# Conditional residual layer: weight-mixing bursts on TensorE in blocks of three, where they stood in blocks of two

## The reference

```python
masked_w = weight * mask[None, :, :]                  # (8, 512, 512)
w_bot = jnp.einsum('bg,got->bot', y, masked_w)         # one 512 x 512 matrix for each batch
return x + jnp.einsum('bnt,bot->bno', x, w_bot) + bias
```

## Time and profile before

| | us |
|---|---|
| median of 3 runs | 605.22 (604.99 to 605.52) |
| the profiled execution | 605.46 |
| its span, first to last instruction | 603.7 |

### The profile page before, as it was taken

How to read it: one execution, slowest core, us unless ns; L and a number is a source line. 1 busy time by engine, 2 the same in 40 slices (tenths; PEclk the granted TensorE clock), 3 DMA queues, 4 the chain that set the end, 5 groups by cost and what they waited for, 6 DMA issues and landing times.

```text
span 603.7 us, 14813 instructions
## 1 busy us (share of the span) xinstructions
PE 592.5 (98%) x6343; PEld 515.9 (85%) x6343; DVE 313.5 (52%) x524; ACT 142.0 (24%) x277; POOL 37.8 (6%) x34
## 2 busy tenths in 40 slices
PE   7899999999999999999999999999999999999998
PEld 6899988888888888888888888888888888888886
DVE  3565535455555555464465465555555555654342
ACT  4443322222222222222222222222222222220000
POOL 3430000000000113221000000000000000000000
PEclk9999999999999999999999999999999999999999
DMA  9976656686776899998766756766767766777952
GB/s 325 406 294 184 207 180 208 219 249 217 239 246 214 290 332 354 343 337 288 238 225 224 250 204 239 249 210 231 246 216 230 234 234 228 227 244 242 298 158 87
DMA packets 61089, 148.59 MB, mean 246 GB/s; under 512 B 6880, under 2 KB 9696, under 8 KB 61024
## 3 DMA queue, kind: packets, MB, share of 16 engines
q1 hardware_dynamic: 40176, 113.00, 57.3%
q10 hardware_dynamic: 20848, 34.64, 15.2%
HBM read 114.07 MB, written 33.55 MB: 245 GB/s over the span
## 4 chain that ended last, share of the span: by engine, by line
PE 95%; DMA 2%; DVE 1%; issue 1%; ACTq 0%; ACT 0%; DVEq 0%
PE ps L438 75%; PE ps L415 20%; DMA bias_sb<-in_bias 1%; DMA xs<-in_mask 1%; DVE wbot L321 0%; DVE staged L335 0%; PE ps L398 0%; ACTq L268 0%; DVE staged L349 0%; ACT wbot L263 0%; DVE wm L189 0%; DVE staged L354 0%; ACTq L277 0%; DVEq L161 0%; DVEq L346 0%
## 5 line engine op out<-in xcount | busy, mean ns | idle before, releaser
L438 PE MATMUL ps<-wbot,xs 128*128 128x256 f32 (+1 forms) x2176 | 459.3, 370 | 4.4 <-DVE wbot L321 3.7
L438 PEld LDWEIGHTS ps<-wbot,xs 128*128 128x128 f32 x2176 | 389.7, 190 | 59.2 <-issue 6.3
L321 DVE COPY wbot<-ps 128x512 f32<-128x512 f32 (+1 forms) x272 | 164.1, 649 | 183.8 <-PE ps L438 174.6
L263 ACT ACTIVATE wbot<-ps 128x512 f32<-128x512 f32 (+1 forms) x276 | 140.7, 568 | 400.7 <-PE ps L415 198.1
L415 PEld LDWEIGHTS ps<-y_sb,wm 32*128 32x128 f32 x4096 | 124.9, 190 | 21.7 <-issue 20.6
L415 PE MATMUL ps<-y_sb,wm 32*128 32x128 f32 x4096 | 137.5, 280 | 2.5 <-DVE wm L189 2.0
L349 DVE TENSOR_TENSOR staged<-ps,staged 128x512 f32<-128x512 f32 x111 | 76.3, 687 | 79.8 <-PE ps L438 79.8
L335 DVE TENSOR_TENSOR staged<-staged,bias_sb 128x512 f32<-128x512 f32 x112 | 76.4, 682 | 0.0
L189 POOL TENSOR_TENSOR wm<-wm,mask_sb 128x512 f32<-128x512 f32 x16 | 20.0, 1270 | 216.3 <-DMA mask_sb<-in_mask 216.3
L349 DVE TENSOR_TENSOR staged<-ps,bias_sb 128x256 f32<-128x256 f32 (+1 forms) x24 | 12.2, 510 | 15.5 <-PE ps L438 11.0
L189 POOL TENSOR_TENSOR wm<-wm,xs 128x512 f32<-128x512 f32 x14 | 17.6, 1274 | 21.7 <-DMA xs<-in_mask 21.4
(11 more groups left out here) (1 smaller groups left out, 0.1 us busy)
## 6 DMA issues: line engine op xcount, KB each, us to landing
xs<-in_x SPq DMA_DIRECT2D x128, 512.0 KB, 3.9
out<-staged ACTq DMA_DIRECT2D x119, 256.0 KB, 4.7
staged<-in_xn SPq DMA_DIRECT2D x112, 256.0 KB, 4.3
wm<-in_w SPq DMA_DIRECT2D x12, 512.0 KB, 6.4
mask_sb<-in_mask SPq DMA_DIRECT2D x8, 512.0 KB, 6.5
out<-staged ACTq DMA_DIRECT2D x18, 128.0 KB, 4.2
wm<-in_w SPq DMA_DIRECT2D x8, 256.0 KB, 6.8
xs<-in_mask SPq DMA_DIRECT2D x4, 512.0 KB, 13.4
```

The source lines that it names most:

```text
L263: eng.activation(tile_place(b, j, first, end), tile_sums(b, j, first, end), ACT.Copy).then_inc(s_ev_a, 1)
L321: eng.tensor_copy(tile_place(b, j, first, end), tile_sums(b, j, first, end)).then_inc(s_ev_v, 1)
L438: ins = eng.matmul(bank[:, at_h:at_h + width], xs[:, n % XRING, h, k, :], at, start=(k == 0), stop=(k == KT - 1))
```

## The change

`bursts_before` is the only function that changes. Before, every even `n` up to 112 had a block of two bursts (`n + 15` and `n + 16`), the first and the last block one burst. Now a unit has blocks ahead of six of its pieces: two bursts ahead of its first and its sixteenth, three ahead of its fourth, seventh, tenth and thirteenth. The blocks of three hold bursts `n + 14`, `n + 15` and `n + 16`. `n` = 0 keeps its single burst, and `n` = 112 has burst 127 alone. The lists `TAKEN` and `BANK_OF` and the loops of all engines follow from the function. The bursts, pieces and copies themselves are the same.

```diff
     n = m - EARLY
     if n == 0:
         return (CS,)
-    return () if n % 2 else tuple(b for b in (n + CS - 1, n + CS) if b < BURSTS)
+    first, count = {0: (-1, 2), 3: (1, 3), 6: (4, 3), 9: (7, 3), 12: (10, 3), 15: (13, 2)}.get(n % GROUPS, (0, 0))
+    at = n - n % GROUPS + CS + first
+    return tuple(b for b in range(at, at + count) if b < BURSTS)
```

## The result

The changed kernel took 629.62 us (median of 4 runs, 627.44 to 630.75) against 605.21 us: a ratio of 1.040 (1.038 to 1.041), 24.4 us more. I had forecast a loss, but 14.7 us of it, and 616 to 628 us as the range. The profiled execution took 629.95 us with a span of 628.2 us.

The account below looks back on a forecast made before the run. The prediction took PE's own instruction stream as the bound. Third-burst waits of 19.6 us less 4.9 us for fewer blocks gave +14.7 on 605.46 profiled, 620.2; the median, 0.24 lower, was forecast at 619.9 us, range 616 to 628.

Parts of the forecast that it names:

- What bounds the kernel: PE's own instruction stream: time taken out is an equal gain, and any wait by PE an equal loss.
- Part 1: Switches between pieces and bursts: 14 fewer blocks at 0.35 us each give back 4.9 us (2.2 to 7.3).
- Part 2, when tile 3's bank comes free: Third burst, steady state: VectorE's copy frees tile 3's bank at +2.67, and the tile starts 0.04 us later.
- all 26 left of the burst wait behind it: Third burst's rest starts 0.72 us late (0.58 in unit 0), 19.6 us over 28 blocks.
- Part 3: Copies, unit-start waits, output and staging loads: all covered, costed at nothing; the load's bias add comes about 11 us on.
- Rival 1: Third burst's 28 waits each end 0.24 us after the copy, not 0.04: 625.5 us; chance 0.12.
- Rival 2: Third burst's banks are free in time, so no wait at tile 3: 600.3 us; chance 0.05.
- Rival 3: Twenty-eight short holes in PE's stream lower the granted clock: about 641 us; chance 0.03.
- What would show it: Profile after: 28 new burst waits of 0.6 to 0.9 us, PE busy time and clock unchanged; new `in_xn` waits contradict.

Follow-up runs that it names:

- experiment 1: The changed kernel with the load into `staged` issued ahead of the second slice's weight and mask loads in SyncE's queue: 624.09 us, ratio 1.031.
- experiment 3: As experiment 1, but ahead of blocks of three VectorE adds the bias behind the copies of the block's first burst: 620.95 us, ratio 1.026.
- experiment 4: As experiment 1, but the first burst isn't copied out in 24 blocks of three, leaving out part of the layer: 603.16 us, ratio 0.997.
- experiment 5: The kernel before with one burst ahead of each piece n = 0 to 111, 112 blocks in place of 57: 715.72 us, ratio 1.183.
- experiment 2: As experiment 1, but a block's third burst waits for all four of its banks before its first matmul: 631.20 us.
- experiment 8: The kernel before with two waits besides the input's, in place of five, ahead of a unit's first and ninth piece: 604.18 us, ratio 0.9982.
- experiment 9: As experiment 8, with VectorE's bias add at unit boundaries moved behind the copies of the block's first burst: 604.26 us, ratio 0.9985.
- experiment 7: The kernel before with only its last burst (127) moved from ahead of piece 112 to ahead of piece 111: 606.08 us, ratio 1.0015.

## Why the prediction was wrong, point by point

The mechanism and the sign were right; 14.7 us were forecast, and 24.4 came. 4.5 us of the difference are a mis-sized term, 5.5 us a step costed at nothing. The first by itself would have left the time inside the range (624.09 us in experiment 1); the second took it out.

- **What bounds the kernel:** right. Every wait and every block saved went into the time one for one (experiments 3 and 4).
- **Part 1, a block is worth 0.35 us:** right, as far as these runs go (13.46 us forecast as 13.49 in experiment 4, 5.55 us against 5.53 in experiment 5). That a change of shape costs something is the trace's answer to the rule of the Trainium skill that I weighed there (TensorE: Matmul & The Clock Gate, Step-by-step: what each phase is for): with weight loads pulled ahead at every change the period would have stayed 13.67 us, and experiment 4 has 13.46.
- **Part 2, when tile 3's bank comes free:** right, +2.67 and 0.04 us more.
- **Part 2, "all 26 left of the burst wait behind it":** here is the mis-sized term. I let the stream go on where it had stopped, so that the block would end 0.72 us late, with 26/32 x 0.91 + 0.19 = 0.93 us to go. It had 1.09 us to go (3.80 - 2.71). The code gives the four tiles four groups of 32 rows, and 0.028 us is the pace of all four together. Tile 3 has all its eight instructions to come when its bank is free, and they take as long as a whole burst, 1.10 us in the earlier trace rows. What the others did before counts for 0.02 us (experiment 2). The wait costs 0.88 us in the steady state and 3.66 - 2.92 = 0.74 in unit 0, 0.16 more than forecast in each: 28 x 0.16 = 4.5 us.
- **Part 3, "the bias add that needs it is two pieces and a block further on, about 11 us":** here is the step that failed. It is true of the one case that I worked out. A load is issued when piece p is done and wanted after the sums of piece p + 2, and in the new order there are cases with no block between: two pieces and VectorE's work, 216.1 to 223.8, 7.7 us. Before, a block of two always lay between, 9.11 us and VectorE's work. And I took the load's time as 4.3 us, the median of the earlier trace rows, where behind the second slice's weights and masks, which I left out, it is 6.7 to 8.2. Either alone was covered: in the kernel before the loads of that stretch landed in 6.8 us (median, 205 to 285 us) and VectorE never waited for one, and in the changed kernel the same short distance led to no wait anywhere else. Together they cost 5.5 us (experiment 1).
- **Rival 1, a slow release:** not so in the changed kernel (0.04 at 227.53 and at 279.01), but its 0.24 is real where waits stand in a row (experiments 2 and 8).
- **Rival 2, free banks:** only in experiment 4, where the copies are left out.
- **Rival 3, the clock:** in part. The 28 short holes did not lower it (1.000 in experiment 1's profile). Behind a hole of 1.69 us at 225 it was 0.50 for some 7 us, and the 48 instructions at 12.81 us and the 26 at 2.07 are 2.25 and 0.92 us of this profile's loss. With the holes gone in experiment 1 the fall is gone too, but one of the changed kernel's four runs had a mean clock of 1.000, and whether the hole stood in that run as well isn't recorded; its 3.4 us over experiment 1 fit the same holes without the fall. That TensorE's clock can swing with idle time between groups of matmuls is what the Trainium skill tells (TensorE: Matmul & The Clock Gate, A second HAM failure mode: psum-queue depth-cycling); here it fell behind one long hole of 1.69 us, and the cycling through banks left it at 1.000.
- **What would show it:** "the waits have a new entry", "PE's busy time hardly moves" and "the clock stays full" were wrong, and the sign named for part 3, new waits for `in_xn`, came. The profile books such a wait inside a burst as busy time of the matmuls around it, and only the count of instructions in narrow stretches, or the length of a block in the chain, shows it.

With both corrections the sum is 14.7 + 4.5 + 5.5 = 24.7 us, against 24.4 measured. The 5.5 is itself a measured difference, so the test of the rest is 14.7 + 4.5 = 19.2 us against experiment 1's 18.9 (624.09 - 605.18).

## What to carry to other kernels

When work is grouped into longer runs to save changes, count the buffers that one run needs: beyond the eight banks the run's length here was the time to the last copy that it needs plus whatever the last tile still has to do, which for these tiles side by side was its whole chain, 1.10 us, not its share of the stream. When the rhythm of one engine changes, take the shortest distance from a load's issue to its use, not the usual one, and set it against the load's time in the busiest stretch of the kernel. In a queue, what is needed soonest goes first, ahead of large loads with time to spare.

## What the runs showed of the hardware that was not expected

- The lag from a copy's end to the matmul that waits for it went with how many waits the code has ahead of it: 0.04 us with one, 0.09 to 0.14 with three (experiments 8 and 9), 0.24 to 0.26 with five or six (experiment 2 and the earlier trace rows, at a burst and at a piece). Which of the waits ends last was not varied.
- After a hole of 1.69 us at 225 us the granted clock fell to 0.50, that is 1.2 GHz. In the kernel before, 2.02 us without a matmul at 4.6 us left it at 1.00; in the profiles of experiments 2 to 5 the clock did fall after that same early hole (1.48 to 2.04 us long), for instance to 0.50 in experiment 4, whose hole had 1.60 us; in experiment 7, with 1.59, it did not. So it isn't the hole's length alone. The changed kernel's timed runs go the same way: 627.44 us at a mean clock of 1.000, 629.30 to 630.75 at 0.992 to 0.995.
